# Attention rows kept by edge, the last stage gathers them by node: one graph layer stack on one core

## The reference

```
deg = max(count of edges into node, 1)
h = x
for l in 0, 1:                                   # relational graph layers
    msg = (rel_embed[type] + h[src]) @ W_r[l]
    agg = segment_sum(msg, dst) * deg**-0.5
    h   = rrelu(agg + (h @ W_sl[l] if node has edges else h @ W_el[l]))
x1  = layernorm(x + h)
# attention block: q of the node, k and v of its source nodes and of itself
e   = sum_per_head(q[d] * k[s]) / 4 ;  alpha = softmax over the edges into d and its own loop
agg = segment_sum(alpha * v[s]) ;  agg = 0 where the node has no edges
x2  = x1 + agg @ Wo + bo
y   = x2 + gelu(layernorm(x2) @ W1 + bf1) @ W2 + bf2
out = layernorm(x1 + y)
```

## Time and profile before

| | us |
|---|---|
| median of 3 runs (2438.11 to 2440.93) | 2438.21 |
| the profiled execution, its own time | 2436.44 |
| its span, first to last instruction | 2434.7 |
| granted TensorE clock, mean over the span | 0.962 |
| TensorE busy | 2066.7 (85%) |
| VectorE busy | 1912.1 (79%) |
| ScalarE busy | 1330.5 (55%) |
| GpSimd busy | 1228.3 (50%) |

### The profile page before, as it was taken

One profiled execution on the slowest core, in us unless ns is written; L12 is line 12 of the kernel. 1 busy time (PEld: TensorE's weight loads), 2 busy tenths in 40 slices (PEclk: granted clock), 3 DMA queues, 4 the chain that ended last, 5 costly groups with the idle time before them and its releaser, 6 DMA issues. The chain is left out here.

```text
span 2434.7 us, 49516 instructions
## 1 busy us (share of the span) xinstructions
PE 2066.7 (85%) x14383; PEld 1685.0 (69%) x14383; DVE 1912.1 (79%) x7786; ACT 1330.5 (55%) x3176; POOL 1228.3 (50%) x1418
## 2 busy tenths in 40 slices
PE   3777777759997888849999399992999999999998
PEld 2555555559997888737776289881777777777776
DVE  3999999978885889869997877773777777777774
ACT  1899999933332455568886200001556666566665
POOL 2764444247772777667772157775333333333332
PEclk9999999989998999979999699996999999999999
DMA  3888888779997688655552156664133333333321
GB/s 85 259 259 242 243 244 241 212 216 292 295 287 242 197 231 237 185 153 164 162 161 75 48 144 195 202 200 152 54 110 111 105 105 105 109 110 108 105 96 53
DMA packets 353686, 413.33 MB, mean 170 GB/s; under 512 B 51340, under 2 KB 235040, under 8 KB 353418
## 3 DMA queue, kind: packets, MB, share of 16 engines
q1 hardware_dynamic: 315850, 339.88, 44.3%
q0 software_dynamic: 34496, 69.37, 11.4%
q10 hardware_dynamic: 3072, 0.92, 0.2%
HBM read 263.50 MB, written 179.89 MB: 182 GB/s over the span
## 5 line engine op out<-in xcount | busy, mean ns | idle before, releaser
L1807 PEld LDWEIGHTS p_y<-w,g_T 128*128 128x128 f32 x3136 | 365.4, 192 | 46.4 <-issue 24.2
L1807 PE MATMUL p_y<-w,g_T 128*128 128x128 f32 x3136 | 365.8, 275 | 0.0
L1825 ACT ACTIVATE nT<-p_n 128x512 f32<-128x512 f32 x98 | 58.5, 597 | 560.3 <-PE p_n L1815 560.3
L1800 PE MATMUL p_f<-nT,w 128*128 128x512 f32 x784 | 354.0, 594 | 0.0
L1790 POOL TENSOR_TENSOR rstd<-var,minus_half 128x4 f32<-128x4 f32 x98 | 113.8, 1161 | 450.3 <-ACT res L1838 450.1
L547 POOL DMA_INDIRECT x_dst<-in_x_dram,idx x196 | 192.2, 981 | 226.9 <-DMA edge_x<-x_dst 144.3
L1832 ACT ACTIVATE g_T<-p_f,bf 128x512 f32<-128x512 f32 x392 | 266.7, 680 | 31.1 <-PE p_f L1800 31.0
L901 POOL DMA_INDIRECT h_src<-h_table,idx x196 | 189.5, 967 | 104.1 <-issue 58.6
L1800 PEld LDWEIGHTS p_f<-nT,w 128*128 128x128 f32 x784 | 141.9, 191 | 141.4 <-issue 141.4
L1597 POOL DMA_INDIRECT x_rows<-xv,idx x196 | 195.6, 998 | 77.8 <-issue 55.2
L1130 POOL DMA_INDIRECT x_src<-x_rows,idx x196 | 184.9, 943 | 85.4 <-issue 55.5
(11 more groups left out here) (321 smaller groups left out, 5548.6 us busy)
## 6 DMA issues: line engine op xcount, KB each, us to landing
xs<-x_rows SPq DMA_DIRECT2D x98, 512.0 KB, 3.7
x_in<-in_x_dram SPq DMA_DIRECT2D x98, 256.0 KB, 4.1
h_table<-h_rows SPq DMA_DIRECT2D x98, 256.0 KB
x_rows<-x_in SPq DMA_DIRECT2D x98, 256.0 KB, 2.9
out_dram<-res SPq DMA_DIRECT2D x98, 256.0 KB, 2.1
x_rows<-x_rows SPq DMA_DIRECT2D x50, 500.0 KB
edge_x<-x_dst SPq DMA_DIRECT2D x98, 128.0 KB, 2.6
h_own<-edge_x SPq DMA_DIRECT2D x49, 256.0 KB, 6.2
```

What stands on the lines that cost most here:

```text
L1800: e.matmul(p_f[ch][:], w_1[:, ch * P:(ch + 1) * P], nT[:, g % 2, :], start=True, stop=True).then_inc(f_prod, 1)
L1807: mm = e.matmul(p_y[g % 2][:, a * D:(a + 1) * D], g_T[:, g % 2, ch, a * P:(a + 1) * P], w_2[:, ch, :], start=(ch == 0), stop=(ch == FCH - 1))
```

## The change

- The pair table shrinks. `x_rows` holds one row per node and the edge rows behind them. A new table `pair_rows` has a pair (`x1`, attention row) for each of the 25088 edges, and a new table `node_place` has one int32 for each node: the place of the edge that ends the node's run, 60000 where there is none.
- The copy of the whole table in layer 0 is gone. Instead seven DMAs of 3584 rows, issued at the start of softmax, copy the edge rows of `x1` into the first half of the pairs.
- `node_place` is filled with 60000 in prepare, and 196 indirect DMAs of 128 places of 4 bytes write the ends: 49 of them from GpSimd's list in dense, 147 in weighted.
- weighted no longer loads `x1` and no longer scatters. The attention row goes from PSUM through ScalarE to a plain store by edge. `w_src` and `w_own` are added on VectorE, and one matmul per tile takes the place of two; the own part therefore enters at the end of a run alone (`end_col`). `bo` is folded into the bias. At the end of the block `node_place` is read into `place_in` by eight DMAs.
- ffn loads `x1` and a broadcast of `bo` into the two halves of `xs`, and GpSimd gathers pairs over them with four indirect DMAs per group by `place_in`; nodes without edges are skipped. GpSimd's epsilon additions go to VectorE, and its two powers become one on 8 columns.
- Everywhere `bn_stats` runs over two rows at once, interleaved, so that its even and odd statistics are those of the two rows; all `bn_aggr` are gone. In dense one of the three row tiles on ScalarE goes to VectorE (`ON_ACT = 2`).

```diff
-    x_rows = nc.dram_tensor("x_rows", [2 * N + EDGES, D], F32).ap()
+    x_rows = nc.dram_tensor("x_rows", [N + EDGES, D], F32).ap()
+    pair_rows = nc.dram_tensor("pair_rows", [EDGES, 2, D], F32).ap()
+    node_place = nc.dram_tensor("node_place", [N, 1], I32).ap()
+        PLACED_EARLY = 49
+        def scatter_place(e, t):
+            return e.indirect_dma_start(out=node_place, in_=edge_place[:, t:t + 1], in_offset=None,
+                                        out_offset=bass.IndirectOffsetOnAxis(ap=idx[:, AT_END, t:t + 1], axis=0),
+                                        bounds_check=N - 1, oob_is_err=False)
...
# dense
-                ON_ACT = 3
+                ON_ACT = 2
+                        if m % 2 and m // 2 < PLACED_EARLY:
+                            scatter_place(e, m // 2).then_inc(placed, 16)
-                            for a in range(GT):
-                                ins = e.bn_stats(stats[:, g % 2, a, :], x_in[:, g % XN, a, :])
+                            for r in range(GT // 2):
+                                ins = e.bn_stats(stats[:, g % 4, r, :, :].rearrange("p w k -> p (w k)"),
+                                                 x_in[:, g % XN, 2 * r:2 * r + 2, :].rearrange("p w d -> p d w"))
-                            for a in range(GT):
-                                ins = e.bn_aggr(mv[:, g % 4, a, :], stats[:, g % 2, a, :])
...
# layer 0
-                        if l == 0 and n < CHUNKS:
-                            e.dma_start(both_table[n * RUN:(n + 1) * RUN, X2, :], both_table[n * RUN:(n + 1) * RUN, X1, :]).then_inc(copied, 16)
...
# softmax
+                    for q in range(7):
+                        part = slice(q * (EDGES // 7), (q + 1) * (EDGES // 7))
+                        e.dma_start(pair_rows[part, X1, :], x_rows[N:N + EDGES, :][part, :]).then_inc(pairs_in, 16)
...
# weighted
-                                e.matmul(p_att[g % 2][:, at], w_src[:, g % 2, j, :], mate[:, g % 2, at], start=True, stop=False)
-                                mm = e.matmul(p_att[g % 2][:, at], w_own[:, g % 2, j, :], ident[:], start=False, stop=True)
+                                mm = e.matmul(p_att[g % 2][:, at], w_sum[:, g % 2, j, :], mate[:, g % 2, at], start=True, stop=True)
-                    for g in range(GE):
-                        e.wait_ge(row_ready, g + 1)
-                        for j in range(GT):
-                            t = g * GT + j
-                            e.indirect_dma_start(out=both_table.rearrange("n a d -> n (a d)"),
...
+                    for t in range(PLACED_EARLY, T):
+                        scatter_place(e, t).then_inc(placed, 16)
+                    for g in range(GE):     # ScalarE
+                        e.wait_ge(out_prod, g + 1)
+                        wait(e, stored[g % ON], 16 * (g // ON))
+                        e.activation(att_out[:, g % ON, :], p_out[g % 2][:], ACT.Copy).then_inc(row_ready, 1)
+                    e.wait_ge(placed, 16 * T)      # SyncE, behind the last store
+                    for first in range(0, NG - 1, SLICE):     # SLICE = 14
+                        last = min(first + SLICE, NG - 1)
+                        e.dma_start(place_in[:, first:last, :],
+                                    node_place[first * GROUP:last * GROUP, :].rearrange("(g p a) o -> p g (a o)", p=P, a=GT)).then_inc(places_in, 16)
...
# ffn
-                            e.dma_start(xs[:, g % XN, :, :, :].rearrange("p a w d -> p (a w d)"),
-                                        rows(both_table, g).rearrange("(p a) w d -> p (a w d)", a=GT)).then_inc(xs_loaded[g % XN], 16)
+                            e.dma_start(xs[:, g % XN, :, X1, :], rows(x_rows, g).rearrange("(p a) d -> p a d", a=GT)).then_inc(xs_in[g % XN], 16)
+                            e.dma_start(xs[:, g % XN, :, ATT, :], bo_rows[:].unsqueeze(1).to_broadcast([P, GT, D])).then_inc(xs_in[g % XN], 16)
+                            e.wait_ge(xs_in[g % XN], 32 * (g // XN + 1))      # GpSimd
+                            for a in range(GT):
+                                e.indirect_dma_start(out=xs[:, g % XN, a, :, :].rearrange("p w d -> p (w d)"), out_offset=None,
+                                                     in_=pair_rows.rearrange("n w d -> n (w d)"),
+                                                     in_offset=bass.IndirectOffsetOnAxis(ap=place_in[:, g, a:a + 1], axis=0),
+                                                     bounds_check=EDGES - 1, oob_is_err=False).then_inc(gathered[g % GN], 16)
+                        m = n - 1
+                            e.wait_ge(var_ready, m + 1)
+                            e.tensor_tensor(rstd[:, m % 4, kinds, :], var[:, m % 2, kinds, :],
+                                            minus_half[:].rearrange("p (k a) -> p k a", k=2)[:, kinds, :], ALU.pow).then_inc(rstd_ready, 1)
```

More of the change, by code:

```diff
@@ L1895, in _ @@
[L1895 to L1901 removed]
+                            x1 = xs[:, g % XN, :, X1, :]
+                            e.tensor_tensor(x1, x1, xs[:, g % XN, :, ATT, :], ALU.add).then_inc(pair_ready, 1)
```

423 lines of the change are left out of this document (207 added, 216 removed).

## The result

Before 2438.33 us (median of 4 runs, 2438.11 to 2440.93), after 2396.86 us (4 runs, 2392.83 to 2399.50): ratio 0.9826, 95% interval 0.9809 to 0.9843, so 1.7% faster, 41.5 us. The forecast was 2367, 71 us less. The profiled execution of after is one of 2399.5 us with a span of 2397.8. Both are needed, because some blocks differ between them.

A forecast was written before the change was run, and what follows sets the result against it. Limits differ by block: VectorE in dense, TensorE in layer 0, weighted and ffn. From 2436.4 us, +0.5 - 17.6 - 8 - 1 - 5 + 0 - 52 + 12 = -71 gave 2365, stated as 2367; own range 2350 to 2382, whole 2335 to 2415.

The forecast's parts named there:

- Dense, -17.6 forecast: Dense: VectorE's list is the limit and gets 0.18 us shorter per step, -17.6 us over 98 steps.
- rival A: Dense and attention: wide statistics cost double, dense gains 6 us and attention 0, whole kernel 2384 us; chance 0.10.
- the 49 place scatters join 220 gathers on GpSimd ... 0: Dense: 269 operations at 1.3 take GpSimd 350 of 445 us, and what waits behind them had long waits already; cost 0.
- Layer 0, -8: Layer 0: without the table copy TensorE gains 4 us at the start and 4 in small waits, -8 (0 to -14).
- Layer 1 and attention, -6: Layer 1 -1 us, paced by its gathers; attention -5, as the destination side's four statistics were put in its pacing loop.
- rival D: Ffn: VectorE operations with two SBUF inputs hold up GpSimd's gathers, 8.87 us per group, +144, 2511 us; chance 0.07.
- Rival C: Softmax and ahead of ffn: small transfers are slow, `place_in` 40 us and copies late by 8, +35, 2402 us; chance 0.11.
- Weighted, -52: Weighted: TensorE's step falls from 4.98 to 4.08 us, then exposed `place_in` loads of 13 us; -52 (-65 to -20).
- Ffn, +12: Ffn: 8.9 us for first gathers and landing, 2 for later groups, 1 for jitter; +12 (+5 to +40).
- and their landing, 3.7: Ffn's start: behind the first load come four gathers, 5.2 us, and 3.7 us until their rows land, +8.9.
- rival B: Ffn: GpSimd paces mildly, power 2.32 and gathers 1.35 give 7.87 us per group, +46, 2413 us; chance 0.14.
- that sign of the forecast: Ffn: after the change GpSimd would be seen waiting for VectorE's variance, with 7.40 us per group.

The follow-up runs named there:

- e3: Changed kernel with dense's 49 place scatters moved behind the early gathers, one in each of steps 24 to 72; 2388.5 us, ratio 0.9802 to the kernel before.
- e12: Changed kernel with a 64 B line per node's place, table fill beside dense, places loaded per group in ffn; 2397.2 us, ratio 0.9819 to the kernel before.
- e6: Changed kernel with dense's 49 place scatters moved, 12 behind layer 0's gathers and 37 into softmax; 2406.1 us, ratio 0.9877 to the kernel before.
- e9: Changed kernel with all 196 scatters writing 64 B pieces to another table, so ffn's gathers move nothing; 2368.9 us, ratio 0.9712 to the kernel before.
- the second profile: Later profile of the changed kernel run again with nothing edited, span 2384.3 us; that run 2389.5 us, ratio 0.9813 to the kernel before.

## Why the prediction was right, and where its steps were wrong

The direction, the order of size and most of the places were right, and the time lies in the stated range. The forecast itself was 30 us too low: 2396.9 lies outside the 2350 to 2382 that had been given to it with 0.56, and inside the range only because that was drawn wide enough for the rivals. Here is where.

**Dense, -17.6 forecast, -2 measured.** Two errors. The list of VectorE was sized nearly right (`bn_stats` 0.65 for 0.64 a pair, so rival A did not happen; the tile that moved 0.28 for 0.23, which is most of the step's 4.41 for 4.35): without scatters dense takes 450.3 us, -13. The other 11.4 are the step "the 49 place scatters join 220 gathers on GpSimd ... 0". I priced the scatters by GpSimd's time and asked who waits behind them there; e3 and e12 show that this was rightly nothing (with 64 B pieces, in steps as full for GpSimd, dense loses nothing). What they cost is the time of the 16 DMA engines, which I had not looked at for them: the earlier trace rows has the share in dense at 0.82, and a 4 B piece holds up what is beside it, as the copies of e6 show. In the changed kernel that costs dense time in steps 10 to 40 alone. The Trainium skill, "DMA: Bandwidth & Descriptors", "Specifications", says that below 512 B a DMA engine reads, modifies and writes. The 4 B pieces agree in direction; the 64 B pieces of e9 and e12 (share 70.7% and 65.1%, against 64.3% without scatters) lie below that limit as well and cost 3 us and nothing in dense, so a limit at 512 B is not what the runs show. Whether it is the size of 4 B, or that neighbours write into one line of memory, the two runs don't separate.

**Layer 0, -8, measured -10.** The block's first matmul after the change:

```profile
513.63 3.51 PE L960 MATMUL p_rel<-rel,onehot 128*128 128x128 f32 x16 [17.62 <-DVE onehot L1007]
```

It comes 6.3 us into the block, where it had been 8.1 (the forecast's 9 is from the window's start at 509.0, the block began at 510.0). That is 2 us of the 10. The other 8 came behind it: from the first to the last start of that product TensorE took 242.4 us before and 234.4 after (234.6 in the second profile), so what the forecast called small waits, 4 us, was worth twice that, and the start half of its 4.

**Layer 1 and attention, -6, measured +3 and +0.5.** ScalarE's root in attention answers to the earlier trace rows:

```profile
1290.07 0.29 ACT L1234 ACTIVATE std<-stats,eps 128x8 f32<-128x8 f32 x1
...
1295.47 0.29 ACT L1234 ACTIVATE std<-stats,eps 128x8 f32<-128x8 f32 x1
```

5.40 us for 5.39: the statistics are not in the loop that paces it, the step of the forecast that put them there was wrong. In layer 1 GpSimd's 196 gathers had a mean of 0.991 us instead of 0.967, 4.7 us in all, as much as the block's 4.5; in the second profile 0.977, 2.0 us in all, for the block's 1.8. 19 of them took over 1.2 us instead of 7, and all of these 26 ran beside VectorE's addition of two SBUF operands. That fits rival D's mechanism, in a block where I had not looked for it; no experiment tested it there, so it is not shown.

**Softmax, 0.** The copies took 42 us for 47 and were covered, and the loads of `place_in` took 10 us and not 40. Rival C did not happen.

**Weighted, -52, measured -50 and -55.** The loop ended 230 and 226 us behind the block's start for 225 forecast, and 221 in the runs with wide pieces; so it, too, lost 5 to 9 us to the scatters, and the forecast had that much of slack elsewhere: the eight loads took 8.0 us to issue and 1.5 us of waiting, where 13 with their landing had been said. So part of the hit is luck, two errors that cancel. The forecast's side sum for these loads, 8 us, is luck too: it divides by 16 engines what the page of the Trainium skill ("DMA: Bandwidth & Descriptors", "Measured (HBM→SBUF, 128 partitions, SWDGE, issued from GpSimd)") works out as the span of a whole transfer over its 64 packets.

**Ffn, +12, measured +23 and +14.** The start: TensorE's third group comes 34.7 us behind the first load instead of 18.4, +16.3 for +11. The step that failed is "and their landing, 3.7": the landing of the first two groups took 5.4 to 5.5 us, and the normalisation of a group stands behind the next group's gathers, which I did not follow in VectorE's list. The pace: the power cost what was taken: 1.7 us in 60 cases and 2.0 in 32, for 1.7. I had counted 7.0 for the cycle with gathers of 1.305; with the issue they took 1.38, and the cycle 7.24 on average. This is rival B in part: the gathers were longer than its 1.35, the power was not its 2.32, and a price was paid only in some executions, 9.4 us in the first profile and none in the second. GpSimd did wait for VectorE's variance (46 us in all) in the first profile too, so that sign of the forecast was there together with the long steps. The sign was not a good one: the two wait for each other in turn. On the power, the Trainium skill's 2.6 cycles per element ("GPSIMD Engine Reference", "3.1 Elementwise — side-by-side cycle accounting") do not carry over from the addition that the page measured: four more columns cost 0.63 us (1.05 to 1.68), not 10 ns.

The sum of what the spans miss, in the order dense, layer 1 with attention, ffn, softmax with weighted, layer 0, prepare: 15.3 + 8.9 + 11.1 + 1.7 - 1.9 - 0.9 = 34 us in the first profile, 18.0 + 6.5 + 1.7 - 2.7 - 2.2 - 0.6 = 21 in the second.

## What to carry to other kernels

Price an indirect DMA three times: the issuing engine's time, its landing, and what its pieces do to the DMA engines. A scatter of single words costs those beside it time as well, here 0.23 us each in dense and 0.86 beside the copies; give each word a line of its own, and then look at who pays for filling and reading the larger table, since a queue that belongs to a compute engine holds that engine up. Look also at where in a block the time is lost: the larger part of dense carried its scatters for nothing. And when an engine's cycle comes within a few per cent of the pacing engine's, expect both outcomes: take several profiles before you read a gain from one, and look at single steps, not at the mean.

## What the hardware did that was not expected

- 37 scatters of 128 four-byte words beside a DRAM-to-DRAM copy of 12.8 MB brought it from about 310 to 175 GB/s (42 to some 74 us); one in every second step of dense raised the hardware queue's share from 64% to 81% for the same bytes (150 to 250 us), and to 89% later on, where it cost no time.
- The same kernel ran ffn's 95 steps at 7.443 or, with twelve longer ones among them, at 7.54 us on average, by the profile; GpSimd's mean gather was longer (1.145 us) in the faster case and its power shorter (1.62 for 1.72).
- Most of a gather's landing at ffn's start is not its data: with every index out of bounds VectorE got the first group 4.5 us behind its last gather, 5.5 with the rows. The fourth group took 1.2 and 1.7 us.
- A queue took 31.9 us to issue 15 DMAs of 125 pieces of 1600 B, and the engine that owns it did nothing in that time.
